# A dynamic convolution on one core: the first pair's statistics, root and weights rearranged

## The chip, the core and the metric

The kernel runs on one core of a Trainium2 chip. The time is that of one execution on the device, in microseconds (us), and a kernel's time is the median of its runs. The engines are TensorE (PE, with its weight loads as PEld), VectorE (DVE), ScalarE (ACT), GpSimd (POOL) and SyncE (SP), which issues nearly all DMAs.

## The reference

```
g   = group_norm(x)                   # x: 32 images, 64 channels, 56 x 56, fp32; groups of 2 channels
a   = relu(mean_hw(g) @ fc1.T + b1)   # 4 values an image
att = softmax(a @ fc2.T + b2)         # 4 values an image
w   = sum_k att[k] * weight[k]        # an own 64 x 64 x 3 x 3 kernel for each image
out = x + conv3x3(g, w, pad 1) + att @ bias
```

## The kernel before

Two images form a pair: image 0 on partitions 0 to 63, image 1 on 64 to 127, so x of a pair is a tile of 128 x 3136. There are 16 pairs. The precision of fp32 is reached with fp16 halves: the scaled input is `xh` + `xl`, the mixed weights are `wh` + `wl`, and each group of output rows adds up three kinds of products, `xh*wh`, `xh*wl` and `xl*wh`. Each product is 64 x 64 x up to 392 columns, and four of them (two images, two regions of rows) share the array. A pair has 4 groups of rows, 9 taps, 3 kinds and 4 quadrants: 432 products. A "third" of the weights is one row of three taps.

Before pair p can be convolved, a chain of small steps has to be done: statistics of each 448-pixel chunk (`bn_stats`, seven a pair), their aggregate per channel, the swap of neighbouring channels (`stream_shuffle`), mean and variance of the group of two, the root `rstd` (GpSimd's `pow`, then one Newton step on VectorE), `sums`, two small products on TensorE (`image_sums`, placed among the products of the pair before by `SUMS_AT`: kind, group, tap step), the logits, the exponentials `ex` on ScalarE, the mixture of the four kernels on VectorE (`share`, `scale_step`, `params_step`, `add_residual`), and its rounding to `wh` on ScalarE (`high_weights_part`) and to `wl` on VectorE (`low_weights`). ScalarE also makes `xh` and takes the results out of PSUM; GpSimd makes the second half of `xl` for the first four pairs.

The order on each engine is written by hand, and semaphores alone join the engines. In pair 0 there is nothing to hide the chain behind: TensorE runs products of ones (`keep_warm`, in numbers of `WARM_PRODUCTS`) up to its first real product. For pair 0, x arrives in seven DMAs of one chunk; the weights are asked for when chunk 4 has landed, and pairs 1 to 3 when the first kernel of the weights has. The scale of the first mixture needs a bound on the weights: the largest magnitude of kernels 0 and 1, by `largest_weights` on VectorE (one of the three reductions stands in the time in which GpSimd takes the root, L389), and `first_range` on TensorE. ScalarE rounds pair 0's input in eight strips of 392 columns (`high_strip`), and takes over two shares of the mixture (`first_share`). TensorE takes pair 0's high products third by third over three groups (`PART_ORDERS`), then all low weights, then the low inputs.

Of the kernel before, what the change touches and what calls it, by code (L numbers as in the profile page):

```python
# [6 lines left out]
B, C, H, W, K, TAPS = 32, 64, 56, 56, 4, 9  # L7
PAIRS = B // 2
# [22 lines left out]

XSCALE = 512.0
WLIMIT = 32768.0
EPS = 1e-5

# [7 lines left out]

FIRST_STRIPS = (1, 4, 2, 6)

X_RING = 4
WARM_PRODUCTS = (54, 10, 10, 6, 6, 4)
# [5 lines left out]
SUMS_AT = ((1, 2, 3), (1, 2, 2), (1, 2, 2), (1, 2, 2), (1, 0, 8), (1, 0, 1), (0, 2, 6), (0, 2, 4), (1, 0, 2))  # L53
SUMS_LATER = (1, 0, TAPS)
LED = 7
PART_ORDERS = (((0, 0), (0, 1), (0, 2), (1, 0), (1, 1), (1, 2), (2, 0), (2, 1), (2, 2)),
               ((0, 0), (0, 1), (1, 0), (1, 1), (0, 2), (1, 2), (2, 0), (2, 1), (2, 2)))
# [25 lines left out]
def shares(p, n=0):  # L83

    return n * K - max(0, n - 1) if p == 0 else K * (mixtures(p - 1) + n) - 2
# [3 lines left out]
def dynamic_conv(nc, x, w_t, small, out):  # L89
# [7 lines left out]
    with ctx:  # L97
# [24 lines left out]
        minus_half = sb("minus_half", [P, 1])  # L122
        b1_part = sb("b1_part", [P, K])
        warm = sb("warm", [P, 1])
        wpart = sb("wpart", [P, 1])
        wbound = sb("wbound", [P, 1])
        wparts = sb("wparts", [P, 3])

        stats = sb("stats", [P, CHUNKS, 6])
        mv = sb("mv", [P, 2])  # L130
        mv_other = sb("mv_other", [P, 2])
        diff = sb("diff", [P, 1])
        diff2 = sb("diff2", [P, 1])
        vsum = sb("vsum", [P, 1])
        vhalf = sb("vhalf", [P, 1])
        var = sb("var", [P, 1])
        root = sb("root", [P, 1])
        newton = sb("newton", [P, 2])
        rstd = sb("rstd", [P, 1])
        pooled = sb("pooled", [P, 1])  # L140
# [26 lines left out]
        s_var = sem("s_var")  # L167
        s_root = sem("s_root")
        s_range = sem("s_range")
        s_std = sem("s_std")  # L170
        s_const = sem("s_const")
        s_warm = sem("s_warm")
        s_wpart = sem("s_wpart")
        x_chunk = [sem(f"x_chunk{n}") for n in range(CHUNKS)]
# [60 lines left out]
        def _(sp):  # L235
# [25 lines left out]
            for n in range(CHUNKS):  # L261
                pixels = slice(n * CHUNK, (n + 1) * CHUNK)
                sp.dma_start(x_sb[0][:, pixels], x_d[0, :, pixels]).then_inc(x_chunk[n], 16)  # L263
# [27 lines left out]
        def _(pool):  # L291
            nc.gpsimd.memset(ones[:], 1.0)
            nc.gpsimd.memset(minus_half[:], -0.5)
            nc.gpsimd.memset(scale[:], 1.0 / WLIMIT)
# [12 lines left out]

            def take_root(p):
                pool.wait_ge(s_var, p + 1)
                nc.gpsimd.tensor_tensor(root[:], var[:], minus_half[:], ALU.pow).then_inc(s_root, 1)  # L310
# [14 lines left out]
            for p in range(PAIRS):  # L325
                take_root(p)
                if p < EARLY:
                    second_low_inputs(p)

        @block.vector  # L330
        def _(dve):
# [5 lines left out]

            def chunk_stats(p, start=0, end=CHUNKS):
                for t in range(start, end):
                    if p == 0:  # L340
                        dve.wait_ge(x_chunk[t], 16)
# [3 lines left out]
                    ins = nc.vector.bn_stats(stats[:, t, :], x_sb[p % X_RING][:, t * CHUNK:(t + 1) * CHUNK])  # L345
                if end == CHUNKS:
                    ins.then_inc(s_stats, 1)

            def channel_means(p):
                dve.wait_ge(s_stats, p + 1)  # L350
                if p >= 1:
                    dve.wait_ge(s_norm, p)
                nc.vector.bn_aggr(mv[:], stats[:]).then_inc(s_aggr, 1)  # L353
                dve.wait_ge(s_aggr, p + 1)

                swap = [n ^ 1 for n in range(32)]
                nc.vector.stream_shuffle(mv_other[:], mv[:], swap).then_inc(s_mv, 1)

            def largest_weights(n):

                dve.wait_ge(s_weights[min(n, 1)], 16)
                half = TAPS * C // 2
                piece = (w_sb[:, 0, :], w_sb[:, 1, 0:half], w_sb[:, 1, half:TAPS * C])[n]
                nc.vector.tensor_reduce(wparts[:, n:n + 1], piece, AX.X, ALU.max,  # L364
                                        apply_absolute_value=True).then_inc(s_wparts, 1)

            def group_stats(p):

                tt, ts, stt = nc.vector.tensor_tensor, nc.vector.tensor_scalar, nc.vector.scalar_tensor_tensor
                n, i = 9 * p, p % 2  # L370
# [5 lines left out]
                dve.wait_ge(s_mv, p + 1)  # L376
# [4 lines left out]
                tt(diff[:], mv[:, 0:1], mv_other[:, 0:1], ALU.subtract).then_inc(gch, 1)  # L381
                glink(n + 2, tt(vsum[:], mv[:, 1:2], mv_other[:, 1:2], ALU.add))
                ts(vhalf[:], vsum[:], 0.5, EPS, ALU.mult, ALU.add).then_inc(gch, 1)
                glink(n + 4, stt(out=diff2[:], in0=diff[:], scalar=0.25, in1=diff[:], op0=ALU.mult, op1=ALU.mult))
                tt(var[:], diff2[:], vhalf[:], ALU.add).then_inc(s_var, 1)  # L385

                ts(gm[i][:], diff[:], -0.5, mv[:, 0:1], ALU.mult, ALU.add).then_inc(gch, 1)
                if p == 0:
                    largest_weights(0)  # L389
                elif p + 1 < PAIRS:  # L390
                    chunk_stats(p + 1, 0, 1)
                dve.wait_ge(s_var, p + 1)
                dve.wait_ge(s_root, p + 1)
                glink(n + 6, ts(newton[:, 0:1], root[:], root[:], var[:], ALU.mult, ALU.mult))  # L394
                glink(n + 7, ts(newton[:, 1:2], newton[:, 0:1], -0.5, 1.5, ALU.mult, ALU.add))
                glink(n + 8, tt(rstd[:], root[:], newton[:, 1:2], ALU.mult))  # L396
                ts(pooled[:], diff[:], 0.5, rstd[:], ALU.mult, ALU.mult).then_inc(gch, 1)

                stt(out=std[i][:], in0=var[:], scalar=1.0 / WLIMIT, in1=rstd[:], op0=ALU.mult,
                    op1=ALU.mult).then_inc(s_std, 1)  # L400
                dve.wait_ge(gch, n + 9)
                if p == 0:
                    dve.wait_ge(s_const, 4)
                    dve.wait_ge(s_small, 16)
                else:

                    dve.wait_ge(s_fc1, 2 * p)
                stt(out=sums[:, 0:K], in0=small_sb[:, FC1:FC1 + K], scalar=pooled[:], in1=b1_part[:],  # L408
                    op0=ALU.mult, op1=ALU.add)
                if p == 0:  # L410

                    stt(out=sums[:, RANGE:RANGE + 1], in0=var[:], scalar=1.0 / WLIMIT, in1=rstd[:], op0=ALU.mult,
                        op1=ALU.mult).then_inc(s_sums, 1)
                else:
                    dve.wait_ge(s_std, p + 1)
# [3 lines left out]
                ts(xof[i][:], gm[i][:], -XSCALE, rstd[:], ALU.mult, ALU.mult).then_inc(s_norm, 1)  # L419
# [11 lines left out]
            def scale_step(p, k):  # L431
# [4 lines left out]
                elif k == 1:  # L436
# [4 lines left out]
                    if p == 0:  # L441
                        dve.wait_ge(s_range, 1)
                        nc.vector.scalar_tensor_tensor(
                            out=wrange[:], in0=tiny[0][:, WEIGHTS:WEIGHTS + 1], scalar=total, in1=exsum[:],
# [19 lines left out]
            def add_residual():  # L464
                centre = mix[:, CENTRE * C:(CENTRE + 1) * C]
# [24 lines left out]

            def mixture_in_parts(p):

                dve.wait_ge(s_exp, p + 1)
                if p >= 1:
                    dve.wait_ge(s_wh, mixed(p - 1))
                for n, part in enumerate(PARTS):
                    if p >= 1 and n == 2:
                        last_quarter(p)
                    done = shares(p, n)
                    for k in range(K):  # L500
                        if p == 0 and n > 0:
                            if k == 0:

                                dve.wait_ge(s_share, n)
                            else:
                                share(p, k, part, done + k - 1)
                        else:
                            if p == 0 and k == 2:
                                dve.wait_ge(s_weights[2], 16)
                            share(p, k, part, done + k)  # L510
# [8 lines left out]
            def first_range():  # L519
                dve.wait_ge(s_wparts, 3)  # L520
                nc.vector.tensor_reduce(wpart[:], wparts[:], AX.X, ALU.max).then_inc(s_wpart, 1)

            def weights_bound():

                dve.wait_ge(s_range, 1)
                nc.vector.tensor_scalar(wbound[:], tiny[0][:, WEIGHTS:WEIGHTS + 1], 1.0 / C, None,
# [26 lines left out]
            def params_step(p, k):  # L553

                n, i = LINKS * p, p % 2
                if k == 0:
# [4 lines left out]
                    if p == 0:  # L561
                        nc.vector.tensor_scalar(par[0][:, 0:1], tiny[0][:, WEIGHTS:WEIGHTS + 1], total, 1.0 / XSCALE,
# [21 lines left out]
            channel_means(0)  # L584
            group_stats(0)
            largest_weights(1)
            logits(0)
            largest_weights(2)
            first_range()
            mixture_in_parts(0)  # L590
            normalise_first_quarter()
            low_weights(0)
            weights_bound()
            dve.wait_ge(s_scaled, 1)
            low_inputs(0, 0)
            chunk_stats(1)
            channel_means(1)
            group_stats(1)
            for p in range(1, EARLY):
# [7 lines left out]
                channel_means(p + 1)  # L607
                group_stats(p + 1)
            for p in range(EARLY, PAIRS):
# [4 lines left out]
                if p + 1 < PAIRS:  # L614
                    chunk_stats(p + 1, 2, 3)
# [395 lines left out]
```

## Time and profile before

| | |
|---|---|
| three runs | 308.75, 309.03, 310.32 us; median 309.03 |
| the profiled execution | 308.6 us, its span 306.8 us |
| busy, of the span | PE 97%, PEld 86%, DVE 80%, ACT 61%, POOL 8% |
| chain of waits, share of the span | PE 93%, DVE 2%, DMA 2%, ACT 1% |

Times in the profile count from the span's start. A row of the timeline gives the start, the length, the engine, the line, the operation, what it writes and reads, and how many were merged; in brackets stands the idle time of the engine before it and what ended it. A product's length holds its way through the array, so rows of products overlap: what counts is how far their starts are apart.

### The profile page before, as it was taken

How to read it: one execution, taken by the hardware profiler on the slowest of the kernel's cores; microseconds unless marked ns; L12 is line 12 of the kernel's file. 1: busy time of each engine (PE TensorE's matmuls, PEld its weight loads, DVE VectorE, ACT ScalarE, POOL GpSimd, SP SyncE). 2: the span in 40 equal slices, each digit the busy share in tenths (PEclk: the TensorE clock that was granted, in tenths of full speed). 3: DMA queues.
4: the chain of work that ended last, by engine and by line, in shares of the span. 5: the costliest groups of instructions: out<-in, count | busy, mean ns of one | idle time of the engine just before them, and what ended most of it. 6: DMA issues, size and time to landing. Idle time of an engine off the chain costs nothing.

```text
span 306.8 us, 15852 instructions
## 1 busy us (share of the span) xinstructions
PE 298.9 (97%) x7068; PEld 263.5 (86%) x7068; DVE 244.3 (80%) x764; ACT 187.1 (61%) x242; POOL 23.4 (8%) x36
## 2 busy tenths in 40 slices
PE   8789999999999999999999999999999999999995
PEld 6557998789987997789977777799999999999884
DVE  3998897979999998888898989878696978856000
ACT  1292929467292938558296868677784866768222
POOL 1005040220500000000000000000000000000000
PEclk9999999999999999999999999999999999999999
DMA  6892864947577575848646767595757352332333
GB/s 206 309 417 95 230 169 130 261 104 224 165 216 182 148 223 129 242 139 220 179 134 163 240 174 252 160 252 148 220 136 216 101 148 64 109 94 77 100 114 102
DMA packets 31444, 53.62 MB, mean 175 GB/s; under 512 B 6800, under 2 KB 24080, under 8 KB 31376
## 3 DMA queue, kind: packets, MB, share of 16 engines
q1 hardware_dynamic: 31152, 52.52, 58.5%
q8 instruction: 55, 0.90, 1.2%
q14 instruction: 13, 0.11, 0.2%
q10 hardware_dynamic: 224, 0.09, 0.1%
HBM read 26.89 MB, written 25.69 MB: 171 GB/s over the span
## 4 chain that ended last, share of the span: by engine, by line
PE 93%; DVE 2%; DMA 2%; ACT 1%; issue 1%; SPq 0%; DVEq 0%
PE acc L855 92%; DMA x<-x 2%; DVE stats L345 1%; ACT xh L670 1%; DVE wparts L364 0%; PE tiny L823 0%; SPq L263 0%; ACT wh L708 0%; ACT mix L714 0%; DVE o L635 0%; DVE mv L353 0%; DVE newton L394 0%; DVE sums L408 0%; DVE logit L428 0%; DVE rstd L396 0%
## 5 line engine op out<-in xcount | busy, mean ns | idle before, releaser
L855 PE MATMUL acc<-xh,wh 64*64 64x385 f16 (+5 forms) x2304 | 111.8, 325 | 0.9 <-ACT wh L708 0.9
L855 PE MATMUL acc<-xh,wl 64*64 64x385 f16 (+5 forms) x2304 | 111.4, 325 | 0.0
L855 PE MATMUL acc<-xl,wh 64*64 64x385 f16 (+5 forms) x2304 | 111.2, 325 | 0.0
L855 PEld LDWEIGHTS acc<-xh,wh 64*64 64x64 f16 x2304 | 86.3, 107 | 12.2 <-ACT wh L708 1.6
L855 PEld LDWEIGHTS acc<-xh,wl 64*64 64x64 f16 x2304 | 87.8, 107 | 10.0
L855 PEld LDWEIGHTS acc<-xl,wh 64*64 64x64 f16 x2304 | 88.0, 107 | 9.6
L734 ACT ACTIVATE o<-acc,par 128x392 f32<-128x392 f32 (+1 forms) x64 | 42.8, 669 | 55.2 <-PE acc L855 55.2
L345 DVE BATCH_NORM_STATS2 stats<-x 128x6 f32<-128x448 f32 x112 | 65.1, 615 | 4.5 <-DMA x<-x 4.5
L682 ACT ACTIVATE xh<-x,xof,xsc 128x1568 f16<-128x1568 f32 x24 | 40.5, 1690 | 31.3 <-DVE xof L419 31.3
L543 DVE TENSOR_TENSOR xl<-x,xh 128x1568 f16<-128x1568 f32 x28 | 49.8, 1783 | 7.7 <-ACT x L645 7.6
L460 DVE SCALAR_TENSOR_TENSOR mix<-w_sb,ex,mix 128x192 f32<-128x192 f32 (+1 forms) x72 | 44.0, 611 | 0.5
L734 ACT ACTIVATE o<-acc,crossed 128x392 f32<-128x392 f32 (+1 forms) x63 | 42.2, 670 | 0.0
L645 ACT ACTIVATE x<-x,xof,xsc 128x1568 f32<-128x1568 f32 x20 | 33.7, 1685 | 0.0
L310 POOL TENSOR_TENSOR root<-var,minus_half 128x1 f32<-128x1 f32 x16 | 8.8, 550 | 191.8 <-DVE var L385 191.8
L322 POOL TENSOR_TENSOR xl<-x,xh 128x840 f16<-128x840 f32 (+1 forms) x8 | 13.2, 1678 | 50.4 <-DVE xl L543 50.4
L635 DVE TENSOR_SCALAR o<-acc,crossed 128x280 f32<-128x280 f32 x1 | 0.6, 569 | 19.4 <-PE acc L855 19.4
L695 ACT ACTIVATE wh<-mix,wsc 128x576 f16<-128x576 f32 (+2 forms) x13 | 9.5, 738 | 8.7 <-DVE mix L466 8.7
L534 DVE SCALAR_TENSOR_TENSOR wl<-mix,wsc,wh 128x576 f16<-128x576 f32 x16 | 12.9, 808 | 1.6 <-ACT wh L695 1.4
L835 PE MATMUL acc<-ones 128*128 128x256 f16 x90 | 12.6, 307 | 1.3 <-POOL eye L296 1.3
L425 DVE SCALAR_TENSOR_TENSOR prod<-tiny,small_sb 128x20 f32<-128x20 f32 x16 | 2.8, 174 | 13.0 <-PE tiny L823 13.0
L458 DVE TENSOR_SCALAR mix<-w_sb,ex 128x576 f32<-128x576 f32 (+1 forms) x22 | 9.3, 422 | 4.4 <-ACT ex L719 4.3
L835 PEld LDWEIGHTS acc<-ones 128*128 128x128 f16 x90 | 9.7, 111 | 3.6 <-POOL eye L296 1.3
(64 smaller groups left out, 143.3 us busy)
## 6 DMA issues: line engine op xcount, KB each, us to landing
x<-x SPq DMA_DIRECT2D x48, 392.0 KB, 4.3
out<-o SPq DMA_DIRECT2D x61, 196.0 KB, 3.8
out<-o SPq DMA_DIRECT2D x122, 98.0 KB, 2.9
x<-x SPq DMA_DIRECT2D x6, 784.0 KB, 9.6
x<-x SPq DMA_DIRECT2D x7, 224.0 KB, 5.0
w_sb<-w_t SPq DMA_DIRECT2D x2, 288.0 KB, 3.1
w_sb<-w_t SPq DMA_DIRECT2D x1, 576.0 KB, 5.4
crossed<-par SPq DMA_DIRECT2D x32, 0.5 KB, 2.5
```

The source lines that it names most:

```text
L322: nc.gpsimd.tensor_tensor(xl[i][:, start:end], x_sb[p][:, start:end], xh[i][:, start:end], ALU.subtract).then_inc(done, 1)
L345: ins = nc.vector.bn_stats(stats[:, t, :], x_sb[p % X_RING][:, t * CHUNK:(t + 1) * CHUNK])
L458: ins = nc.vector.tensor_scalar(**columns, scalar1=ex[:, 0:1], scalar2=None, op0=ALU.mult)
L460: ins = nc.vector.scalar_tensor_tensor(**columns, scalar=ex[:, k:k + 1], in1=mix[:, part], op0=ALU.mult, op1=ALU.add)
L534: nc.vector.scalar_tensor_tensor(out=wl[i][:], in0=mix[:], scalar=wsc[i][:], in1=wh[i][:], op0=ALU.mult, op1=ALU.subtract).then_inc(s_wl, 1)
L543: nc.vector.tensor_tensor(rows_of(xl[i], half), rows_of(x_sb[p % X_RING], half), rows_of(xh[i], half), ALU.subtract).then_inc(s_xl[half], 1)
L645: nc.scalar.activation(v, v, ACT.Identity, bias=xof[i][:], scale=xsc[i][:]).then_inc(s_xn[half], 1)
L682: nc.scalar.activation(rows_of(xh[i], half), rows_of(x_sb[p % X_RING], half), ACT.Identity, bias=xof[i][:], scale=xsc[i][:]).then_inc(s_xh ...
L695: nc.scalar.activation(high[:, rows], mixed_w[:, rows], ACT.Copy, scale=wsc[i][:]).then_inc(s_wh, 1)
L734: nc.scalar.activation(o_sb[i][r][:, at:at + rows * W], acc[n % SLOTS][r][:, 0:rows * W], ACT.Identity, bias=scales[:, 1:2], scale=scales[ ...
L835: nc.tensor.matmul(acc[SLOTS - 1][0][:, 0:2 * P], ones[:].bitcast(fp16)[:, 0:P], ones[:].bitcast(fp16), start=True, stop=True)
L855: ins = nc.tensor.matmul(pixels[:, top:bottom, left:right], weights[i][halves[m], tap * C:(tap + 1) * C], window, start=start and step == ...
```

## The change

- Swap before the means: the chunks' statistics (not the two means) are swapped between neighbouring channels, in pair 0 six chunks before the last chunk's statistics. The group's mean and variance then come from one aggregate over own and swapped statistics; a second, own aggregate gives the difference for `sums`. Epsilon is added to the statistics of chunk 0.
- Root on VectorE: a first guess from the bits of the variance, then two steps, in all pairs. GpSimd's `take_root` goes. The statistics of the next pair's chunk 0, which stood in the wait for it, go behind the group's statistics; in the later pairs the chunks between the logits and the mixture shift by one.
- Weights bounded by their squares: ScalarE sums the squares of kernels 0 and 1 for each partition, GpSimd takes one `pow` of two columns, TensorE adds both up. `largest_weights` goes.
- Pair 0's mixture: the residual is added before the last share, ScalarE takes one share instead of two, the low weights are made part by part, and TensorE takes each third's high products and then its low ones. ScalarE rounds strips 2 and 3, and 6 and 7, in one instruction each.
- x0 arrives in five pieces, of 1, 1, 2, 2 and 1 chunks; the weights are asked for behind the third piece, and pairs 1 to 3 behind the second kernel.
- 46 first warm-up products instead of 54, and other places for pair 1's and pair 4's sums.

```diff
+PIECES = ((0, 1), (1, 2), (2, 4), (4, 6), (6, 7))
+GATE = 2
-WARM_PRODUCTS = (54, 10, 10, 6, 6, 4)
+WARM_PRODUCTS = (46, 10, 10, 6, 6, 4)
-SUMS_AT = ((1, 2, 3), (1, 2, 2), (1, 2, 2), (1, 2, 2), (1, 0, 8), ...
+SUMS_AT = ((1, 2, 6), (1, 2, 2), (1, 2, 2), (1, 1, 8), (1, 0, 8), ...
...
-            sp.wait_ge(x_chunk[4], 16)
+            sp.wait_ge(x_piece[GATE], 16)
             for n, ks in enumerate((slice(0, 1), slice(1, 2), slice(2, K))):
                 sp.dma_start(w_sb[:, ks, :], w_t[:, ks, :]).then_inc(s_weights[n], 16)
-            sp.wait_ge(s_weights[0], 16)
+            sp.wait_ge(s_weights[1], 16)
...
+            pool.wait_ge(s_wsquares, 2)
+            nc.gpsimd.tensor_tensor(wnorms[:], wsquares[:], half_power[:], ALU.pow).then_inc(s_wnorms, 1)
...
+                    if p == 0 and t == CHUNKS - 1:
+                        dve.wait_ge(s_most, 1)
+                        dve.wait_ge(s_eps, 1)
+                        swap_stats(0, 0, CHUNKS - 1).then_inc(s_other, 1)
...
             def group_stats(p):
+                nc.vector.bn_aggr(own[:], stats[:, 0, :]).then_inc(gch, 1)
+                dve.wait_ge(s_other, p + 2)
+                glink(n + 2, nc.vector.bn_aggr(mv[:], stats[:].rearrange("p a b -> p (a b)")))
+                var = mv[:, 1:2]
+                ts(guess[:].bitcast(mybir.dt.int32), var.bitcast(mybir.dt.int32), -0.5, ROOT_BITS, ALU.mult,
+                   ALU.add).then_inc(gch, 1)
+                ts(vhalf[:], var, -0.5, None, ALU.mult)
+                tt(diff[:], own[:, 0:1], mv[:, 0:1], ALU.subtract).then_inc(gch, 1)
+                dve.wait_ge(gch, n + 4)
+                stt(out=square[:], in0=guess[:], scalar=guess[:], in1=var, ...)
+                ts(part_guess[:], guess[:], 0.375, None, ALU.mult)
+                stt(out=series[:], in0=square[:], scalar=-10.0 / 3.0, in1=square[:], ...)
+                stt(out=better[:], in0=series[:], scalar=5.0, in1=part_guess[:], ...)
+                ts(fdiff[:], small_sb[:, FC1:FC1 + K], diff[:], None, ALU.mult)
+                glink(n + 8, stt(out=newton[:], in0=better[:], scalar=better[:], in1=vhalf[:], ...))
+                stt(out=rstd[:], in0=newton[:], scalar=1.5, in1=better[:], ...).then_inc(s_rstd, 1)
...
+                if 1 <= p < PAIRS - 1:
+                    chunk_stats(p + 1, 0, 1)
...
+            def first_mixture():
+                ...
+                share(0, 2, part, 2)
+                scale_step(0, 2)
+                dve.wait_ge(s_part, 3)
+                add_residual()
+                dve.wait_ge(s_mix, 1)
+                share(0, 3, part, 3)
+                for n, part in enumerate(PARTS[1:], 1):
+                    if n == 2:
+                        dve.wait_ge(s_share, 1)
+                    for k in range(n - 1, K):
+                        share(0, k, part, shares(0, n) + k - (n - 1))
+                        if k == n:
+                            low_part(n - 1)
+                        if n == 1:
+                            params_step(0, k)
+                normalise_first_quarter()
+                low_part(2)
...
+            def squares(k):
+                act.wait_ge(s_weights[k], 16)
+                ...
+                nc.scalar.activation(mix[:], w_sb[:, k, :], ACT.Square, scale=DOWN,
+                                     accum_out=wsquares[:, k:k + 1]).then_inc(s_wsquares, 1)
...
             for p in range(EARLY, PAIRS):
+                logits(p)
                 if p + 1 < PAIRS:
                     chunk_stats(p + 1, 1, 2)
-                logits(p)
-                if p + 1 < PAIRS:
-                    chunk_stats(p + 1, 2, 3)
                 mixture(p)
                 if p + 1 < PAIRS:
-                    chunk_stats(p + 1, 3, 5)
+                    chunk_stats(p + 1, 2, 5)
...
+            for k in range(2):
+                squares(k)
+            first_high(1, 2, s_strip)
             exponentials(0)
+            first_high(4, 5, s_strip)
+            first_high(2, 4, s_quarter[1])
+            first_high(5, 6, s_quarter[2])
             high_weights_part(0, 0)
+            first_high(6, 8, s_quarter[3])
+            first_high(0, 1, s_quarter[0])
             first_share(2)
             high_weights_part(0, 1)
+            normalise_quarter(0, 1)
             high_weights_part(0, 2)
...
+            for n in range(len(PARTS)):
+                steps = range(3 * n, 3 * n + 3)
+                pe.wait_ge(s_wh, n + 1)
+                for g in range(SLOTS):
+                    ...
+                    high(0, g, steps)
+                pe.wait_ge(s_wl, n + 1)
+                for g in range(SLOTS):
+                    products(0, g, wl, xh, steps)
```

## Rows read from the trace of the kernel before

**Rows 1.** The page: span, and TensorE's busy time (its share, instructions).
```profile
span 306.8 us, 15852 instructions
...
PE 298.9 (97%) x7068; PEld 263.5 (86%) x7068; DVE 244.3 (80%) x764; ACT 187.1 (61%) x242; POOL 23.4 (8%) x36
```

**Rows 2.** The chain that ended last: start, length, what.
```profile
6.54 2.90 DVE stats L345 x5
...
236.59 17.76 PE acc L855 x431
...
303.39 0.57 DVE o L635
```

**Rows 3.** DMA issues of x0's chunks 2, 3 and 6, and the weights: us to landing.
```profile
x<-x SPq DMA_DIRECT2D x1, 224.0 KB, 4.9
...
x<-x SPq DMA_DIRECT2D x1, 224.0 KB, 5.0
...
x<-x SPq DMA_DIRECT2D x1, 224.0 KB, 5.3
...
w_sb<-w_t SPq DMA_DIRECT2D x2, 288.0 KB, 3.1
```

**Rows 4.** Timeline from 0 to 20 us, all engines.
```profile
0.72 3.24 SPq L263 DMA_DIRECT2D x<-x  x7
...
1.18 1.28 ACT L739 ACT_TABLE_LOAD   x1 [1.18 <-PEq L1004]
...
9.47 0.35 DVE L353 BATCH_NORM_AGGREGATE mv<-stats 128x2 f32<-128x42 f32 x1
...
9.86 0.15 DVE L357 STREAM_SHUFFLE mv_other<-mv 128x2 f32<-128x2 f32 x1
...
10.76 0.74 DVE L364 TENSOR_REDUCE wparts<-w_sb 128x1 f32<-128x576 f32 x1
...
11.56 0.27 DVE L394 TENSOR_SCALAR newton<-root,var 128x1 f32<-128x1 f32 x1
...
12.64 0.15 DVE L412 SCALAR_TENSOR_TENSOR sums<-var,rstd 128x1 f32<-128x1 f32 x1
...
12.85 0.28 PE L823 MATMUL tiny<-sums,ones 64*64 64x6 f32 x4 [2.09 <-DVE sums L412]
...
15.01 1.91 ACT L670 ACTIVATE xh<-x,xof,xsc 128x392 f16<-128x392 f32 x3
...
16.07 0.28 DVE L466 SCALAR_TENSOR_TENSOR mix<-eye,stdx,mix 128x64 f32<-128x64 f32 x1
...
17.32 1.74 PE L855 MATMUL acc<-xh,wh 64*64 64x392 f16 x36 [0.74 <-ACT wh L708]
...
19.22 3.18 PE L855 MATMUL acc<-xh,wh 64*64 64x385 f16 x72 [0.17 <-ACT wh L708]
```

**Rows 5.** Instructions grouped by line and shape: count, busy us, mean ns.
```profile
L460 DVE SCALAR_TENSOR_TENSOR mix<-w_sb,ex,mix 128x192 f32<-128x192 f32 x36 | 14.9, 415 | 0.5
...
L652 ACT ACTIVATE x<-x,xof,xsc 128x784 f32<-128x784 f32 x9 | 8.8, 1026 | 0.0
```

**Rows 6.** Timeline at 23 and 30 us: GpSimd's low inputs, pair 1's sums.
```profile
23.11 3.31 POOL L322 TENSOR_TENSOR xl<-x,xh 128x840 f16<-128x840 f32 x2 [11.66 <-DVE xl L543]
...
29.74 0.15 DVE L417 TENSOR_TENSOR sums<-std,wbound 128x1 f32<-128x1 f32 x1
```

**Rows 7.** Timeline around 88 us: the change from pair 3 to pair 4.
```profile
87.55 1.65 PE L855 MATMUL acc<-xl,wh 64*64 64x385 f16 x34
...
89.15 3.16 PE L855 MATMUL acc<-xh,wh 64*64 64x392 f16 x68
```

**Rows 8.** Stretches of 2 us: busy us and instructions of PE, PEld, DVE, ACT, POOL; clock.
```profile
2.00:4.00 2.00, 2.00 (x11) 1.41 (x10) 0.69 (x2) 0.66 (x2) 0.31 (x2) 1.00 1.03 274
...
6.00:8.00 2.00, 2.00 (x21) 1.80 (x19) 1.46 (x3) 0.00 (x0) 0.00 (x0) 1.00 0.67 250
```

**Rows 9.** VectorE's timeline in pair 9: before its second low inputs.
```profile
161.83 1.79 DVE L543 TENSOR_TENSOR xl<-x,xh 128x1568 f16<-128x1568 f32 x1 [0.61 <-ACT x L645]
```

More of the change, by code:

```diff
@@ L336, in link, with swap_stats @@
                 dve.wait_ge(dch, n)
+            swap = [n ^ 1 for n in range(32)]
+            def swap_stats(p, first, end):
+                columns = slice(6 * first, 6 * end)
+                return nc.vector.stream_shuffle(stats[:, 1, columns], stats[:, 0, columns], swap)
             def chunk_stats(p, start=0, end=CHUNKS):
@@ L346, in chunk_stats, with swap_last_stats @@
                 if end == CHUNKS:
                     ins.then_inc(s_stats, 1)
-            def channel_means(p):
+            def swap_last_stats(p):
                 dve.wait_ge(s_stats, p + 1)
                 if p >= 1:
[L352 to L365, printed above, removed]
+                    dve.wait_ge(s_eps, p + 1)
+                swap_stats(p, CHUNKS - 1 if p == 0 else 0, CHUNKS).then_inc(s_other, 1)
@@ L380, in group_stats @@
                         dve.wait_ge(s_xn[half], p - 1)
[L381 to L401, printed above, removed]
+                ts(gm[i][:], mv[:, 0:1], 1.0, None, ALU.mult)
+                dve.wait_ge(gch, n + 6)
+                stt(out=better[:], in0=series[:], scalar=5.0, in1=part_guess[:], op0=ALU.add,
+                    op1=ALU.mult).then_inc(gch, 1)
                 if p == 0:
@@ L500, in mixture_in_parts @@
                     for k in range(K):
[L501 to L510, printed above, removed]
+                        share(p, k, part, done + k)
                         if n == 0:
@@ L826, in first_range @@
             def first_range():
-                pe.wait_ge(s_wpart, 1)
-                nc.tensor.matmul(tiny[0][:, WEIGHTS:WEIGHTS + 1], scale[:], wpart[:],
-                                 start=True, stop=True).then_inc(s_range, 1)
+                pe.wait_ge(s_wnorms, 1)
+                for k in range(2):
+                    ins = nc.tensor.matmul(tiny[1][:, WEIGHTS:WEIGHTS + 1], scale[:], wnorms[:, k:k + 1],
+                                           start=k == 0, stop=k == 1)
+                ins.then_inc(s_range, 1)
             def keep_warm(n):
@@ L936, in _ @@
                             high(p, g)
-                pe.wait_ge(s_wl, p + 1)
-                for g in range(SLOTS):
-                    low(p, g, 0)
+                if p >= 1:
+                    pe.wait_ge(s_wl, lows(p))
+                    for g in range(SLOTS):
+                        low(p, g, 0)
                 pe.wait_ge(s_xl[0], p + 1)
```

224 lines of the change are left out of this document (118 added, 106 removed).

## The prediction

> **What bounds the kernel now.** I read the page first: one core, span 306.8 us, TensorE busy for 97% of it [rows 1]. The chain of waits then says where that engine is not yet the bound: the first 17 us go through the landing of x0, the statistics and the scalar work on VectorE, and from there to 303.39 the chain is TensorE's products; a pair takes 17.76 us, and the tail behind them is 0.57 us [rows 2]. Sixteen pairs at 17.76 are 284.2 us; from the first product at 17.32 to 303.39 are 286.1. So a change outside the products can win only in two places: the start of the first product (17.3 us), and about 1.9 us inside the stream, part of which is the 0.06 us or so that every pair loses at its image sums.
>
> Where those 1.9 us are: I went along TensorE's timeline. In pair 0 the first 36 products end at 19.06, so the last of them (one lasts 0.33) begins at 18.73, and the next, which waits for the second third of the high weights, at 19.22 [rows 4]: 0.49 us, where four products are 0.16 apart, so 0.33 lost. At the change from pair 3 to pair 4 the last product of pair 3 begins at about 88.87 (the row's 34 products end at 89.20, one product lasts 0.33) and the next pair begins at 89.15, with some 0.12 us more at its second third: together about 0.38 us [rows 7].
>
> Before the first product: seven DMAs of 224 KB are issued every 0.46 us from 0.72; chunk 2 is issued at 1.65 and lands 4.9 us later, at 6.5; chunk 3 5.0 later, at 7.1; the last, issued at 3.5, lands at 8.8 [rows 3]. VectorE starts five statistics at 6.54, one per 0.58 us, and is through at 9.43; it is this engine and chunk 2, not the last chunk, that set 9.43 [rows 2]. Then 3.36 us of scalar steps to the sums at 12.79, and 4.03 more to the first high weights at 16.82: there the mixture was ready at 16.35, but ScalarE was still in its strips until 16.92, the next instruction overlapping by 0.1 [rows 4]. So ScalarE holds the last 0.45 us.
>
> **The change part by part.**
>
> *x0 in five pieces.* Chunks 2 and 3 now land as one. The bytes and the 16 engines are the same, and each piece must wait for the slowest of them, so I let the piece land when chunk 3 does now, 7.0 to 7.1, not at 6.5: +0.5 us at the start of the run of five statistics. Bounds: if chunk 2 was late by accident, the run is set by the last piece instead; at 8.8 for that piece and 0.62 for its statistics the end stays at 9.4, my lower end. The upper end is chunk 4's slot, one more 0.58.
>
> *Work inside that run.* An epsilon is added to chunk 0's statistics (0.08), and the first six chunks' statistics are swapped before the last, behind a wait for their end: 0.15 for the shuffle [rows 4], about 0.1 for the wait. Bounds of this swap: 0.15 (2 columns), 0.35 (the aggregate of 42 columns, read as a shuffle). I take 0.25. Sum: the last statistics end at 9.43 + 0.5 + 0.08 + 0.25 = 10.25.
>
> *Group statistics.* Removed: the hop to GpSimd (written at 10.7, read at 11.56, behind a 0.66 us reduction) and the means of two channels. Added: a second aggregate, over 84 columns, and the root in five dependent steps. An independent small step costs 0.07, a dependent one 0.19, one with a pointer scalar 0.25. From the end of the statistics: 0.13 swap, 0.31 own aggregate, 0.59 joint aggregate (42 columns take 0.35, of which 0.15 is any instruction's; twice 0.20 on top is 0.55, plus 0.04 to be seen; bounds 0.35 and 0.70), 0.33 guess, half, difference, then 0.25 + 0.19 + 0.19 + 0.25 + 0.19 to the root and 0.27 to the sums: 2.70, against 3.36 now. The sums are ready at 10.25 + 2.70 = 12.95, that is 0.16 later than now. Here the pieces eat what the root wins.
>
> *The bound on the weights.* Three reductions on VectorE (0.74, 0.44, 0.44) go; ScalarE, idle till 13.0, takes two squares of 576 columns instead. By 1.03 for 784 columns [rows 5] each is under 1.0. The weights are issued 0.6 us earlier (behind the piece at 7.1, not chunk 4 at 7.67) and take 3.1 us each, 0.45 apart [rows 3]: landed at 10.2 and 10.7, squares done by 11.9, hidden before the normalisation's scales at 13.1. GpSimd's one root (0.57) ends at 12.6, and the range is wanted at 15.1: hidden.
>
> *To the first product.* From the sums the exponentials and first share follow as now, 0.09 sooner because no reduction lies in between: share 0 at 14.36. Shares 0 to 3 with the residual before the last end at 16.43 (now 16.35 after 14.29, the same length). ScalarE has one share less and strips 2 and 3 in one instruction, 1.03 in place of two steps of 0.60, so it is free at 16.4: high weights at 16.47, first product at 16.96. That is **0.36 us earlier**: ScalarE's 0.43 and the 0.09, less 0.16 for the later sums.
>
> *Low weights part by part.* TensorE now does a third's high products and then its low ones, 2.95 us for both, so the second third is wanted at 19.9 and the last at 22.9; they come at 19.1 and 20.9. The 0.33 us of pair 0 go. Three parts of 0.42 in place of one of 0.81 [rows 5], one more share and the queue of waits put VectorE later: its low inputs end at 23.8, not 22.9. Behind them GpSimd needs 0.18 and, for 840 of its 1568 columns, 1.78 of the row's 3.31 [rows 6], to 25.8, and TensorE wants that at 16.96 + 8.88 = 25.84: covered by less than 0.1 us. Next late are pair 1's sums: chunk 0 is already done, six more to 27.2, 2.8 for the chain: 30.0; TensorE comes to the place at 25.84 + 96 products of 0.041 = 29.8 (now the sums are there at 29.89 [rows 6], 0.15 before it comes). I charge **0.2 us of new stall**; 0 and 0.7 are its ends.
>
> *Later pairs.* The chain without GpSimd is 2.84 against 3.25 with one chunk inside. In pairs 0 to 3 that chunk goes behind it, a gain of 0.3; the sums of pair 4 are also taken three taps earlier. That is enough for the gap at 89: **0.38 us off**. From pair 4 one more chunk stands between exponentials and low inputs, but VectorE idles there for ScalarE (0.61 us before the second low inputs [rows 9]), which hides 0.54. In pairs 4 and 5, with no idle time, the sums have 0.4 and 0.8 us in hand.
>
> Sum: -0.36 - 0.33 + 0.2 - 0.38 = **-0.87 us**. The profiled execution took 308.6 us (span 306.8 and 1.8 around it), so 307.7; the median of the runs is 309.03, 0.4 higher, and 0.87 off it is 308.16: I forecast **308.1 us**.
>
> **A rule weighed.** One table load of 1.28 us stands in the trace, and Exp, Identity and Copy all run after it [rows 4]. The trace has no Square. The Trainium skill, "ScalarE: Activation LUTs", section "Table sets: the hidden batching unit", says tables come in named sets, cheap functions are in every set, and a function of another set costs a load; it does not name Square among the cheap ones. By that rule the sum is unchanged if Square is in Exp's set.
>
> **Rivals.**
> 1. *Slower: TensorE's clock falls.* Warm-up products touch at 11 per 2 us at 2 to 4 us and at 21 at 6 to 8 us, with a granted clock of 1.00 in both rows [rows 8]: half pace (1.2 GHz) first, then 2.4 GHz, after 4.4 us of steady products. Now the engine rests for 2.09 us before the sums [rows 4] and keeps its pace. With 46 products, not 54, it stops at 8.4 and waits for the statistics till 10.25, 1.85 us, and after ten products (1.1) again 1.5 us. If that brings half pace, products lose half of 4.4 us: +2.2, giving 310.3, slower than before. It decides if the idle share between 8.4 and 13, 3.4 of 4.6 us against 2.35 of 3.6 now, is too much. Against it: each rest is shorter than one that did no harm. The Trainium skill, "TensorE: Matmul & The Clock Gate", section "HAM oscillation — how this bites in real kernels", says that idle gaps between bursts bring the slower clock back; by its rule too a short rest is harmless.
> 2. *Square brings its own table.* The load before it is hidden in ScalarE's idle time, the one back to Exp stands between strip 1 and the exponentials: 1.28, hence 309.4.
> 3. *Chunk 2's lateness was chance.* Merged pieces let the last piece set the end (9.4): 0.85 us more is won, 307.2.
> 4. *The extra waits eat the gain.* The joint aggregate at 0.70, the swap at 0.35, pair 1's sums late by 0.7, the low inputs late: +0.9, back to 309.0. For it: margins of 0.1 us. Against it: nearly every wait is counted at its measured step.
>
> **How the numbers follow.** Chances: the forecast 0.50, rival 1 0.08, rival 2 0.06, rival 3 0.20, rival 4 0.16. The range takes in rivals 2 to 4 and the bounds of the swap and the landing: 307.0 to 309.7. This kernel's measurement can tell about 0.5%, 1.5 us, from no change: under 307.5 is faster, above 310.6 slower. Rival 3 and the low edge of the forecast give faster 0.27; a clock that rises late, or two mishaps together, slower 0.07; same 0.66.
>
> **What would show it.** Right: in the new trace the second piece lands near 7.0, the last statistics end near 10.25, sums near 12.95, one table load, the first product near 17.0, no gap in pair 0 above 0.05 us until the sums of pair 1 near 30, no gap at pair 4. Wrong: a first product above 17.3, a piece that lands under 6.3, a second table load, products of pair 0 at half pace, or pairs 5 to 15 longer than 17.8 us.

## The result, and the profile after

The changed kernel is slower by 0.5%: 310.26 us median of 20 runs (308.35 to 311.2) against 308.37 of 20 runs of the kernel before, ratio 1.0049 [1.0037, 1.006]. I forecast 308.1 us, within 307.0 to 309.7. By my own bounds (under 307.5 faster, above 310.6 slower) 310.26 still counts as "same" (0.66), but the interval lies wholly on the slower side, and I had forecast a gain. The three runs behind my 309.03 were high draws among the 20: by the median of 20 my gain of 0.87 us means 307.5, so what has to be explained is +1.89 us in place of -0.87. The profiled execution took 311.2 us. Its page and its stretches of 2 us (busy us and instructions of PE, PEld, DVE, ACT, POOL; then the granted clock, the DMA share and GB/s):

```profile
span 309.3 us, 15873 instructions
...
PE 300.9 (97%) x7062; PEld 280.3 (91%) x7062; DVE 248.0 (80%) x813; ACT 188.7 (61%) x243; POOL 15.4 (5%) x21
...
PEclk9869999999999999999999999999999999999999
```

```profile
10.00:12.00 2.00, 0.61 (x6) 0.55 (x7) 1.84 (x8) 0.81 (x3) 0.00 (x0) 1.00 1.06 409
12.00:14.00 2.00, 0.67 (x9) 0.36 (x6) 1.86 (x16) 0.74 (x2) 0.72 (x1) 0.89 0.86 218
14.00:16.00 2.00, 2.00 (x13) 1.48 (x14) 1.26 (x8) 1.66 (x4) 0.00 (x0) 0.50 0.96 391
16.00:18.00 2.00, 2.00 (x12) 1.69 (x11) 1.01 (x6) 1.49 (x2) 0.00 (x0) 0.50 1.04 433
18.00:20.00 2.00, 2.00 (x11) 1.44 (x10) 1.93 (x10) 1.30 (x3) 0.00 (x0) 0.50 0.99 414
```

The reader is to see 0.50 from 14 to 20 us: TensorE runs at 1.2 GHz, at 11 to 13 products in 2 us where 21 fit [rows 8]. The timeline of the same stretch:

```profile
1.28 7.83 PE L891 MATMUL acc<-ones 128*128 128x256 f16 x46 [1.28 <-POOL eye L308]
...
8.21 0.63 DVE L369 BATCH_NORM_STATS2 stats<-x 128x6 f32<-128x448 f32 x1 [3.57 <-DMA x<-x]
...
10.72 0.62 DVE L369 BATCH_NORM_STATS2 stats<-x 128x6 f32<-128x448 f32 x1
11.10 0.68 ACT L767 ACTIVATE mix<-w_sb 128x576 f32<-128x576 f32 x1 [8.43 <-DMA w_sb<-w_t]
...
11.39 1.27 PE L891 MATMUL acc<-ones 128*128 128x256 f16 x10 [2.28 <-DVE stats L369]
...
11.70 0.47 DVE L399 BATCH_NORM_AGGREGATE mv<-stats 128x2 f32<-128x84 f32 x1
...
13.78 0.15 DVE L438 SCALAR_TENSOR_TENSOR sums<-mv,rstd 128x1 f32<-128x1 f32 x1
...
13.98 0.38 PE L877 MATMUL tiny<-sums,ones 64*64 64x6 f32 x4 [1.33 <-DVE sums L438]
...
16.40 0.85 PE L884 MATMUL tiny<-wnorms,scale 128*128 128x1 f32 x4
...
17.12 3.48 PE L891 MATMUL acc<-ones 128*128 128x256 f16 x16
17.29 0.22 DVE L472 SCALAR_TENSOR_TENSOR wrange<-tiny,exsum 128x1 f32<-128x1 f32 x1 [0.99 <-PE tiny L884]
...
18.70 0.46 ACT L754 ACTIVATE wh<-mix,wsc 128x192 f16<-128x192 f32 x1 [1.21 <-DVE mix L489]
...
20.53 1.69 PE L911 MATMUL acc<-xh,wh 64*64 64x392 f16 x36
```

The piece of chunks 2 and 3 lands at 8.2 us, not at 7.0; TensorE rests 2.28 us ahead of its ten products and 1.33 behind them, and the granted clock falls to 0.50 at 13.55 and is back at 20.4. The warm-up products between the sums and the first real product now take twice their time, so that the weights' range (16.40) holds up the mixture, and the last of them hold up the first product: it comes at 20.53, though its weights are ready at 19.16. It came at 17.32 before [rows 4]. The stream from the first product's start to the last one's end is shorter, 285.2 us against 285.9. So 3.2 us are lost ahead of it and 0.7 won in it.

### The profile page after: what moved, and what is told of

Read it like the earlier page. It is cut to its first block, busy times and chain, and to the rows that moved or that the text cites. A ratio compares the mean times of both kernels' runs of the same rounds, so it can differ in the third digit from the quotient of the medians.

```text
span 309.3 us, 15873 instructions
## 1 busy us (share of the span) xinstructions
PE 300.9 (97%) x7062; PEld 280.3 (91%) x7062; DVE 248.0 (80%) x813; ACT 188.7 (61%) x243; POOL 15.4 (5%) x21
## 4 chain that ended last, share of the span: by engine, by line
PE 94%; DVE 1%; issue 0%; DVEq 0%
PE acc L911 92%; PE acc L891 2%; PE tiny L877 0%; DVE stats L369 0%; PE tiny L884 0%; DVE o L683 0%; DVE mv L399 0%; DVE stats L352 0%; DVE own L397 0%; DVE fdiff L423 0%; DVE sums L435 0%; DVE square L407 0%; DVE rstd L426 0%; DVE guess L401 0%; DVE newton L425 0%
## 5 line engine op out<-in xcount | busy, mean ns | idle before, releaser
L911 PE MATMUL acc<-xh,wl 64*64 64x385 f16 (+5 forms) x2304 | 112.6, 325 | 0.0
L911 PEld LDWEIGHTS acc<-xl,wh 64*64 64x64 f16 x2304 | 92.8, 107 | 4.6
L911 PEld LDWEIGHTS acc<-xh,wl 64*64 64x64 f16 x2304 | 92.4, 107 | 4.9
L911 PEld LDWEIGHTS acc<-xh,wh 64*64 64x64 f16 x2304 | 91.0, 107 | 5.7 <-issue 0.3
L891 PE MATMUL acc<-ones 128*128 128x256 f16 x82 | 14.9, 363 | 3.6 <-DVE stats L369 2.3
L891 PEld LDWEIGHTS acc<-ones 128*128 128x128 f16 x82 | 10.5, 132 | 7.1 <-DVE stats L369 2.6
L588 DVE SCALAR_TENSOR_TENSOR wl<-mix,wsc,wh 128x576 f16<-128x576 f32 x15 | 12.1, 805 | 1.1 <-ACT wh L739 1.1
L772 ACT ACTIVATE ex<-logit,nmax 128x4 f32<-128x4 f32 x16 | 4.7, 293 | 11.7 <-DVE nmax L458 11.4
```

Of the source, the lines that this page charges most:

```text
L588: nc.vector.scalar_tensor_tensor(out=wl[i][:], in0=mix[:], scalar=wsc[i][:], in1=wh[i][:], op0=ALU.mult, op1=ALU.subtract).then_inc(s_wl, 1)
L891: nc.tensor.matmul(acc[SLOTS - 1][0][:, 0:2 * P], ones[:].bitcast(fp16)[:, 0:P], ones[:].bitcast(fp16), start=True, stop=True)
L911: ins = nc.tensor.matmul(pixels[:, top:bottom, left:right], weights[i][halves[m], tap * C:(tap + 1) * C], window, start=start and step == ...
```

## The experiments

Each kernel was timed beside the kernel before. Every run gives its mean granted clock; a fall to 0.50 shows as 0.994 or less. All 20 runs of the changed kernel fell: 16 stand at 0.989 (median 310.39), four at 0.994 (median 308.70).

**1. Fill the first rest** (`e1_fill`).

```diff
-WARM_PRODUCTS = (46, 10, 10, 6, 6, 4)
+WARM_PRODUCTS = (66, 10, 10, 6, 6, 4)
```

> The changed kernel with 66 first warm-up products instead of 46, nothing else. Clock theory: the changed kernel lost its time because TensorE rested 2.28 and 1.33 us with only ten products between, its granted clock then stood at 0.50 from 13.6 to 20.4 us, and the warm-up products that stand ahead of the first real one ran at half pace. With the first rest filled the clock stays at 1.00 from about 6 us on, the first product comes at 17.5 to 18.2 us instead of 20.53, and the time falls by 2 to 3 us, from 310.3 to 307.3 to 308.3. Landing theory: the loss is the piece of chunks 2 and 3 that lands at 8.2 us (chunk 2 landed at 6.5 before) and all that follows from it; then the fill changes nothing beyond 0.5 us and the time stays at 309.8 to 310.8.

Measured: 308.3 us (307.7 to 308.82), ratio 0.9991 [0.9981, 1.0001]; all 12 runs at 0.999 or more. Its timeline:

```profile
7.58 0.63 DVE L369 BATCH_NORM_STATS2 stats<-x 128x6 f32<-128x448 f32 x1 [2.84 <-DMA x<-x]
...
13.17 0.15 DVE L438 SCALAR_TENSOR_TENSOR sums<-mv,rstd 128x1 f32<-128x1 f32 x1
13.38 0.28 PE L877 MATMUL tiny<-sums,ones 64*64 64x6 f32 x4 [1.16 <-DVE sums L438]
...
16.92 0.46 ACT L754 ACTIVATE wh<-mix,wsc 128x192 f16<-128x192 f32 x1
17.43 1.69 PE L911 MATMUL acc<-xh,wh 64*64 64x392 f16 x36 [0.46 <-ACT wh L754]
```

With the rest filled the clock stays at 2.4 GHz and 2.0 us come back: the clock theory holds for the loss. The first product of this profile comes 3.1 us sooner than in the changed kernel's, but 0.6 of that is a sooner landing in this one run (7.58 against 8.21). The kernel is then level with the one before, not 0.9 better.

**2 and 3. Seven DMAs again, without and with the fill** (`e2_seven`, `e3_seven_fill`).

```diff
-PIECES = ((0, 1), (1, 2), (2, 4), (4, 6), (6, 7))
-PIECE_OF = (0, 1, 2, 2, 3, 3, 4)
-GATE = 2
+PIECES = tuple((n, n + 1) for n in range(CHUNKS))
+PIECE_OF = tuple(range(CHUNKS))
+GATE = 4
...
+WARM_PRODUCTS = (66, 10, 10, 6, 6, 4)   # e3 alone
```

> The changed kernel with x0 in seven DMAs of one chunk again and the weights asked for behind chunk 4, as before the change; still 46 first warm-up products. Landing theory: the statistics of x0 end about 1 us earlier (near 10.2 instead of 11.3 us) and the time falls by 1 to 2 us, to 308.3 to 309.3, whatever the clock does. Clock theory: the rest ahead of the statistics shrinks from 2.3 to about 1.3 us but two rests remain; where the granted clock still falls (mean 0.989 or 0.994) the time stays above 309, and only runs with a mean clock near 1.00 are at 308 or under.

> Seven DMAs for x0 and 66 first warm-up products: both edits together. Clock theory: the clock stays at 1.00, first product at 16.8 to 17.3 us, 307.2 to 307.8, at most 0.7 us below the kernel with five pieces and 66 products. Landing theory: equal to the kernel with seven DMAs and 46 products within 0.4 us.

Without the fill: 308.33 us, ratio 0.9979 [0.9957, 1.0001], in two groups: five runs at 1.0 have a median of 306.88, seven at 0.994 or less take 307.88 to 309.3 (median 309.11). With it: 307.11 us, 0.9953 [0.9937, 0.9969], no fall in six runs. The rests of the first were 0.89, 1.33 and 0.46 us in its profile, which is of a run that did not fall. So the clock's fall costs 2.2 us here as well, and five pieces instead of seven cost 1.2 us (308.3 - 307.11) that have nothing to do with the clock.

**4 and 5. The warm-up alone, on the kernel before** (`e4_before_46`, `e5_before_66`).

```diff
-WARM_PRODUCTS = (54, 10, 10, 6, 6, 4)
+WARM_PRODUCTS = (46, 10, 10, 6, 6, 4)   # e4; 66 in e5
```

> The kernel before with 46 first warm-up products instead of 54, nothing else: the rest ahead of the statistics grows from 0.27 to about 1.1 us, the one of 2.09 us behind it stays. Clock theory: if two rests with ten products between are what brings the clock down, part of the runs show a mean clock of 0.99 and 1.5 to 3 us more, and the median rises by 0.5 us or more. Landing theory: no change, within 0.3 us of the kernel before.

> The kernel before with 66 first warm-up products instead of 54, nothing else. Clock theory: 10 of the 29 runs of the kernel before also show a mean clock of 0.993 or 0.994 and take 0.7 us more; with the first rest filled none do, all stand at 0.998 or more, and the median is 308.2, at most 0.5 us under the kernel before. So of the 1.6 us by which seven DMAs with the fill beat the kernel before, the fill alone gives at most 0.5 and the rearranged work the rest. Rival: the fill itself is what wins; then this kernel comes to 307.1 as well.

With 46: 309.12 us, ratio 1.0021 [1.0006, 1.0036], and all 12 runs show a fall (six at 0.993 or 0.994, median 308.5; six at 0.989, median 309.58). In its profile the full pace came only at 7.3 us, so the 46 products still reached to the statistics; the one long rest there is the old one of 2.09 us. With 66: 308.45 us, 0.9999 [0.9984, 1.0015]; it wins nothing, and, against what I wrote, 3 of 12 runs still fell. So the fill is not what makes the seven-DMA kernel fast; and the kernel before was itself not safe: beside experiments 1 to 4, 10 of its 29 runs stood at 0.993 or 0.994 and took 0.6 us more (308.94 against 308.35 for the other 19).

**6. Merge chunks 4 and 5 only** (`e6_six_fill`).

```diff
+PIECES = ((0, 1), (1, 2), (2, 3), (3, 4), (4, 6), (6, 7))
+PIECE_OF = (0, 1, 2, 3, 4, 4, 5)
+GATE = 3
...
+WARM_PRODUCTS = (66, 10, 10, 6, 6, 4)
```

> The changed kernel with 66 warm-up products and x0 in six DMAs: chunks 0 to 3 alone, 4 and 5 as one, 6 alone; the weights behind chunk 3. Theory of the wait: a merged piece lands when its second chunk would; chunk 2 is there at 6.0 again, the merged piece at 7.8 to 8.3 where statistics 4 would start at 7.3 with seven DMAs: statistics end 0.5 to 1.0 us later than with seven (9.8 to 10.3), first product 16.5 to 17.0. Theory of the long rows: rows of 3584 bytes come slower as well, as they did for chunks 2 and 3 (median engine 6.1 to 6.8 us against 5.8 to 6.1 for chunk 3 alone); the merged piece lands at 8.7 or later and the statistics end at 10.7 or later.

Measured: 307.87 us, 0.9982 [0.9969, 0.9995], no fall in ten runs.

```profile
5.81 0.63 DVE L369 BATCH_NORM_STATS2 stats<-x 128x6 f32<-128x448 f32 x1 [1.11 <-DMA x<-x]
6.54 0.63 DVE L369 BATCH_NORM_STATS2 stats<-x 128x6 f32<-128x448 f32 x1
8.01 1.16 DVE L369 BATCH_NORM_STATS2 stats<-x 128x6 f32<-128x448 f32 x2 [0.84 <-DMA x<-x]
```

This merged piece lands at 8.0, where chunk 5 alone lands at 7.8 to 8.3: here the merge costs the wait for the second chunk and no more, 0.8 us of idle VectorE and 0.8 us of time against experiment 3.

**7 and 8. Two steps of the prediction inside the stream** (`e7_lows_after`, `e8_sums_pair4`, both on the kernel of experiment 3).

```diff
...
                     high(0, g, steps)
+            for n in range(len(PARTS)):
+                steps = range(3 * n, 3 * n + 3)
                 pe.wait_ge(s_wl, n + 1)
...
```
```diff
-SUMS_AT = ((1, 2, 6), (1, 2, 2), (1, 2, 2), (1, 1, 8), ...
+SUMS_AT = ((1, 2, 6), (1, 2, 2), (1, 2, 2), (1, 2, 2), ...
```

> Seven DMAs and 66 warm-up products, but TensorE takes pair 0's high products of all three thirds first and then the low ones, as before the change. My prediction's step says the thirds in turn hide the making of the second third: then this order shows a gap of 0.5 to 0.9 us ahead of the second third (made at 18.2, wanted at 17.5) and the stream from first to last product grows from 285.2 to 285.7 or more, 307.6 to 308.0. If the order is worth nothing, no such gap and 307.1.

> Seven DMAs and 66 warm-up products, with pair 4's sums taken at the old place (kind 1, group 2, step 2) and not three taps earlier. My prediction's step says that the earlier place removes the gap of 0.28 us at the change from pair 3 to pair 4: then a gap of 0.1 to 0.3 us comes back there. If the shorter chain of statistics alone removed it, the two kernels do not differ there.

Low products last: 307.79 us, 0.9975 [0.9964, 0.9986], 0.7 above experiment 3, with its place in the trace:

```profile
16.39 1.69 PE L911 MATMUL acc<-xh,wh 64*64 64x392 f16 x36 [0.46 <-ACT wh L754]
18.62 2.56 PE L911 MATMUL acc<-xh,wh 64*64 64x385 f16 x52 [0.54 <-ACT wh L754]
```

Pair 4's sums at the old place: 307.4 us, 0.9956 [0.994, 0.9973]. The gap of [rows 7] is back: the last product of pair 3 begins at 87.05 (the first row ends at 87.38, less 0.33) and the next at 87.32, 0.27 later:

```profile
85.73 1.65 PE L911 MATMUL acc<-xl,wh 64*64 64x385 f16 x34
87.32 4.82 PE L911 MATMUL acc<-xh,wh 64*64 64x392 f16 x108
```

In experiment 3, the same kernel with the new place, the two are 0.12 us apart (87.82 and 87.94):

```profile
85.09 1.64 PE L911 MATMUL acc<-xh,wl 64*64 64x392 f16 x36
86.51 1.64 PE L911 MATMUL acc<-xl,wh 64*64 64x392 f16 x36
87.94 4.70 PE L911 MATMUL acc<-xh,wh 64*64 64x392 f16 x108
```

So much lies between any two such rows (86.40 to 86.51 in the same view): the gap itself was worth 0.15 us, and the next 108 products take 0.12 less. Both steps are shown; the second is worth 0.27 us in the traces, and 307.4 (five runs) against 307.11 is within the runs' spread.

**9 and 10. Where the warm-up products should stand** (`e9_lean`, `e10_second_burst`, both on the changed kernel).

```diff
-WARM_PRODUCTS = (46, 10, 10, 6, 6, 4)
+WARM_PRODUCTS = (46, 10, 2, 0, 0, 0)    # e9
+WARM_PRODUCTS = (46, 24, 10, 6, 6, 4)   # e10
```

> The changed kernel with warm-up products 46, 10, 2, 0, 0, 0: the 24 that follow the sums and stand ahead of the weights' range and of the first real product go. Theory of the filler: when the clock is at 0.50, most of the 2.1 us are lost because these products at half pace (0.213 us each, 5.5 us in all) hold up the weights' range and the first product; without them the first product comes at 17.5 to 18.3 us in spite of the half clock, runs at half pace until the clock is back, and the time falls from 310.3 to 308.7 to 309.5 with a mean clock of 0.99 or less. Theory of the products: half pace hurts where it meets real products; then taking the filler away wins nothing, or loses, because the clock stays low longer: 310.3 or more.

> The changed kernel with warm-up products 46, 24, 10, 6, 6, 4: the rest ahead of the statistics (2.28 us) stays, the one behind them (1.33 us) is filled. If the sum of the rests decides, 2.3 us in all is like the kernel before and the seven-DMA kernel with 46 (2.4 and 2.2 us; the clock fell in a third and in half of their runs): the clock falls in 20 to 60% of the runs and the median is 308.3 to 310. If the first, long rest alone decides, it falls in all runs and nothing is won: 310.3. If a full second burst is enough, no falls and 308.3.

Without the filler: 310.18 us, ratio 1.0054 [1.0034, 1.0074]. My theory of the filler failed. The first product does come at 17.49, but the first 36 take 3.08 us instead of 1.69, and five of seven runs stand at 0.982 or 0.983, lower than any run of the changed kernel. The other two, at 0.988, took 309.51 and 309.95, 0.7 us less than the changed kernel's runs at 0.989, so what the missing filler saves is lost again where the clock stays low for longer. The profile is of one of these two:

```profile
17.49 3.08 PE L911 MATMUL acc<-xh,wh 64*64 64x392 f16 x36 [2.85 <-ACT wh L754]
```

With the second rest filled: 309.27 us, 1.0019 [0.9999, 1.004]; six runs fell (median 310.24), six did not (308.55). The profile is of a run that fell: TensorE rests 2.85 us until 11.44, and the clock falls at 12.5, one microsecond into the second burst. So the first rest alone can bring the fall; filling the second one spares half of the runs, and filling the first one (experiment 1) all of them.

**11 and 12. Five pieces in the kernel before; the best version again** (`e11_before_five`, with 66 warm-up products; `e12_best` is the kernel of experiment 3).

```diff
+PIECES = ((0, 1), (1, 2), (2, 4), (4, 6), (6, 7))
...
+WARM_PRODUCTS = (66, 10, 10, 6, 6, 4)
...
-            sp.wait_ge(x_chunk[4], 16)
+            sp.wait_ge(x_chunk[2], 16)
...
```

> The kernel before with the change's five pieces for x0 (weights behind the third piece) and 66 first warm-up products, against its own 308.4 with 66 and seven DMAs. Pieces theory: merging chunks 2 and 3 makes the first run of statistics begin at 7.6 to 8.2 instead of 6.2 us, in this kernel as in the changed one: +1.0 to 1.5 us, 309.4 to 309.9. Rival: the late landing comes with something else of the change (less issued work, other traffic), then no difference above 0.4 us.

> The changed kernel with seven DMAs and 66 warm-up products once more, beside the others on one chip: 306.8 to 307.4, 1.2 to 1.8 us under the kernel before, no clock below 0.997. If its first result was a draw of the chip, it comes to 308 or more.

Five pieces in the kernel before: 310.35 us, 1.006 [1.0038, 1.0082], 1.9 over the same kernel with seven (308.45); the rest ahead of its sums is 2.09 us as ever, and five of six runs fell. The sixth, at a full clock, was the slowest of them (311.37); nothing on record says why.

```profile
7.51 2.79 DVE L347 BATCH_NORM_STATS2 stats<-x 128x6 f32<-128x448 f32 x5 [2.87 <-DMA x<-x]
...
13.71 0.28 PE L825 MATMUL tiny<-sums,ones 64*64 64x6 f32 x4 [2.09 <-DVE sums L414]
```

So the pieces bring the loss by themselves, and more falls with it than the 3 of 12 of the same kernel with seven DMAs, though on another chip. The best version, no fall in its six runs: 306.91 us, 0.9944 [0.9927, 0.9961], on another chip than experiment 3: 1.6 us under the kernel before, in both trials.

```profile
6.42 0.63 DVE L369 BATCH_NORM_STATS2 stats<-x 128x6 f32<-128x448 f32 x1 [1.84 <-DMA x<-x]
...
12.05 0.15 DVE L438 SCALAR_TENSOR_TENSOR sums<-mv,rstd 128x1 f32<-128x1 f32 x1
...
15.80 0.45 ACT L754 ACTIVATE wh<-mix,wsc 128x192 f16<-128x192 f32 x1
16.30 1.69 PE L911 MATMUL acc<-xh,wh 64*64 64x392 f16 x36 [0.46 <-ACT wh L754]
```

**13 and 14. Why the merged piece is late** (`f1_rows`, `f2_size`, on the kernel of experiment 1).

```diff
+                for part in halves if end - first == 2 else (slice(0, P),):          # f1
+                    sp.dma_start(x_sb[0][part, pixels], x_d[0, part, pixels]).then_inc(x_piece[n], 16)
...
+PIECE_OF = (0, 1, 2, 3, 2, 3, 4)          # f2
...
+            for n, ts in enumerate((slice(0, 1), slice(1, 2), slice(2, 5, 2), slice(3, 6, 2), slice(6, 7))):  # f2
+                sp.dma_start(x_t[:, ts, :], x_dt[:, ts, :]).then_inc(x_piece[n], 16)
```

> The changed kernel with 66 warm-up products; chunks 2 and 3, and 4 and 5, still in rows of 3584 bytes with one wait for both, but as two DMAs of 64 partitions each: seven DMAs of 224 KB. In the profiles so far the merged piece of chunks 2 and 3 lands at 7.4 to 8.2 us, chunk 3 alone at 6.5 to 7.2. Long rows theory: rows of 3584 bytes are what comes late: the piece lands at 7.4 or later, 308.0 or more. Size theory: one DMA of 448 KB is what comes late, the rows do not matter: the piece lands at 6.4 to 7.2 and the time is 307.3 to 307.9.

> The changed kernel with 66 warm-up products and five DMAs of the same sizes as in the change, but the two of 448 KB carry chunks 2 and 4, and 3 and 5, so that every row is 1792 bytes. Long rows theory: the piece with chunk 2 lands at 6.4 to 7.2 and the statistics end at 9.5 to 10.2. Size theory: it lands at 7.4 or later, as with chunks 2 and 3 in one, and the statistics end at 10.6 or later, 308.0 or more.

Long rows in small DMAs, then short rows in large ones:

```profile
6.75 0.63 DVE L370 BATCH_NORM_STATS2 stats<-x 128x6 f32<-128x448 f32 x1 [2.14 <-DMA x<-x]
7.34 0.62 DVE L370 BATCH_NORM_STATS2 stats<-x 128x6 f32<-128x448 f32 x1
9.14 1.15 DVE L370 BATCH_NORM_STATS2 stats<-x 128x6 f32<-128x448 f32 x2 [1.18 <-DMA x<-x]
```

```profile
7.56 0.63 DVE L369 BATCH_NORM_STATS2 stats<-x 128x6 f32<-128x448 f32 x1 [2.92 <-DMA x<-x]
8.69 1.68 DVE L369 BATCH_NORM_STATS2 stats<-x 128x6 f32<-128x448 f32 x3 [0.45 <-DMA x<-x]
```

The long rows' first piece is in time (6.75), the short rows' large one is late (7.56): for this piece the size of the DMA counts, not the rows. Yet the times are equal, 308.45 and 308.42, because with small DMAs of half the partitions the second pair of chunks comes at 9.14. One of the ten runs of experiment 14 fell (309.72), none of experiment 13.

A DMA is complete when all its 16 parts have landed, and the kept traces hold the time of each. The 16 parts of the large piece come in from 5.2 to 8.2 us in the changed kernel, the last alone 1.0 us behind the rest, and from 5.0 to 7.5 in experiment 14; those of chunk 3 alone in experiment 3 from 5.3 to 6.6. So it is the late parts that make the piece late. One rival was not tested: five DMAs are all issued by 3.0 us, seven by 4.0, so the pieces behind the large one are under way sooner as well. Why its last parts are late stays open; there is one profile of each.

## Why the prediction was wrong

*The rest of TensorE: the step that failed.* Rival 1 said what happened and got 0.08, on the sentence "each rest is shorter than one that did no harm". Three things were wrong in it. The rests were 2.28 and 1.33 us, not 1.85 and 1.5: the landing was later by more than the 46 products were, which end at 9.1 and not at 8.4, because the full pace began later. It began at 5.7 us in the profile that I had read, and anywhere from 4.3 (experiment 11) to 7.5 (experiment 14) in the others. One rest was weighed against one rest, though only 1.27 us of products lay between the two. And that the kernel before "keeps its pace" was read from one profile, while 32 of its 96 runs beside the experiments fell: its rests were not harmless.

The shares of runs with a fall, with TensorE's rests ahead of the first real product (ahead of the fall for experiment 9) in one profile each: the changed kernel 20 of 20 (3.6 us) and experiment 9 7 of 7 (2.9), experiment 10 6 of 12 (3.3), experiment 2 7 of 12 (2.7), experiment 11 5 of 6 (2.4), the kernel before a third (2.9), experiment 14 1 of 10 (1.7), experiments 1, 3, 6, 7, 8 and 12 none of 49 (1.8 or less). Longer rests in all go with more falls, but the sum does not decide: experiment 13 has 2.85 us and no fall in 10 runs, experiment 4 has 2.2 and only falls, experiment 5 1.3 and 3 falls in 12. The shares also differ between chips (the kernel before fell in 3 of 19 runs beside experiments 13 and 14, in 24 of 59 beside 1 to 8), and the rests of runs that were not profiled are unknown. The condition is not settled. The Trainium skill, "TensorE: Matmul & The Clock Gate", section "HAM oscillation — how this bites in real kernels", warns of one gap longer than any here; the falls in these runs do not agree with it as it stands.

The price, 2.2 us, was right in size (310.39 at 0.989 against 308.3 for experiment 1, 2.1). That rival 1's 310.3 meets the measured 310.26 is partly luck: its base, 308.1, stood on the high draw of 309.03, and the part of the landing that was left out made up for it. The price's mechanism was partly another: in the profile it is the warm-up products that are slow and in the way, but experiment 9 shows that they cannot simply be left out.

*The landing of the merged piece: a term mis-sized.* I took +0.5 us, with 1.1 as the upper end. The run of five statistics begins at 8.2 us in the changed kernel, 7.4 to 8.3 in experiments 1, 9, 10 and 11, against 6.5 [rows 2] and 5.9 to 6.4 in seven further profiles with seven DMAs: 7.8 against 6.2 on the mean, +1.6 us. In time it is 1.2 us at a full clock, 0.7 more than I charged, and so nearly the whole of the missing gain: -0.87 was forecast, and experiment 1 is level. With the clock's 2.0 us that makes 2.7 of the 2.76 us between forecast and result. Without the pieces my sum would have read -1.37 us, and seven DMAs bring -1.2 and -1.5 at a full clock (307.11 against 308.35, 306.91 against 308.45).

*What held.* Epsilon and early swap: 0.33 forecast; from the start of chunk 2's statistics to the end of the last it takes 3.19 us in experiments 3 and 12, against 2.89 in the kernel before. The chain from statistics to sums: 2.70 forecast, 2.59 measured (11.34 to 13.93), 3.36 before; the joint aggregate took 0.47. The squares are hidden, though they end at 12.75 and not at 11.9, as the weights are asked for behind the late piece (8.21), and no second table load appears: rival 2 is out. From the sums to the first product: 4.01 forecast, 4.10 at a full clock (experiment 12: 12.20 to 16.30), 4.53 before. Low weights part by part: 0.33 forecast; taking them last costs 0.7 us. Pair 4: 0.38 forecast, 0.27 measured by experiment 8; I had counted as a gap what lies between any two rows. The 0.2 us of stall at pair 1's sums did not come. The stream is 0.7 us shorter, 0.51 forecast.

## What to carry to other kernels

Count a filler that keeps TensorE's clock against the latest, not the usual, arrival of what ends it, and look at all rests ahead of the first real product together; read the clock of many runs, as one profile shows one draw. A merge of DMAs on the path to the first result moves the first byte's use to the last byte's landing, and here more than that: measure the landing itself. When a change bundles a dozen edits, two cheap ones (the pieces and 46 instead of 54) can hide that the others win 1.2 to 1.5 us at an equal clock.

## What was not expected of the hardware

One DMA of 448 KB issued at 1.63 us landed at 7.4 to 8.3 us in six profiles, where two of 224 KB, issued at 1.63 and 2.10, both landed by 6.5 to 7.2.

The clock of TensorE fell in all 20 runs of the changed kernel, in whose profile no single rest was over 2.3 us, and in a third of the runs of the kernel before, whose profile (of a run that did not fall) has rests of 2.09 and 0.74 us.

With the products behind the sums left out (experiment 9) it stayed low for more of the run in five of seven runs: a mean of 0.982 against 0.989.
